# Layer 1 of a graph stack: row ends made per graph as small products of two one-hots and spread over the heads by DMA

## What is computed

```python
g_l = (h @ W_l.T).reshape(b, n, H, F)
g_r = (h @ W_r.T).reshape(b, n, H, F)
g_sum = g_r[:, :, None] + g_l[:, None]              # one vector for each pair (i, j)
e = einsum('bijhf,f->bijh', leaky_relu(g_sum, 0.2), w_attn)
e = where(adj == 0, -inf, e)
a = softmax(e, axis=j)
attn = einsum('bijh,bjhf->bihf', a, g_r)
out = leaky_relu(attn, 0.2)
```

## Time and profile before

| | |
|---|---|
| profiled execution | 1467.18 us |
| its span, first to last instruction | 1465.5 us |
| mean granted TensorE clock | 0.976 |
| PE busy | 1370.2 us, 93% |
| PE weight loads | 1154.1 us, 79% |
| DVE busy | 1150.3 us, 78% |
| ACT busy | 999.2 us, 68% |
| POOL (GpSimd) busy | 121.0 us, 8% |
| DMA queue of SP | 365.81 MB, 70.3% of 16 engines |

### The profile page before, as it was taken

How to read it: one execution, slowest core, us unless ns; L and a number is a source line. 1 busy time by engine, 2 the same in 40 slices (tenths; PEclk the granted TensorE clock), 3 DMA queues, 4 the chain that set the end, 5 groups by cost and what they waited for, 6 DMA issues and landing times. The chain is left out here.

```text
span 1465.5 us, 27752 instructions
## 1 busy us (share of the span) xinstructions
PE 1370.2 (93%) x9135; PEld 1154.1 (79%) x9194; DVE 1150.3 (78%) x2223; ACT 999.2 (68%) x2538; POOL 121.0 (8%) x259
## 2 busy tenths in 40 slices
PE   7984999999999999999999988799999999999867
PEld 6873666888888888888888887588888888888767
DVE  5875778787878878878788564589998989898967
ACT  5754878656566666666666421688888888888746
POOL 2011000000000000000000000000010001001176
PEclk9997999999999999999999999899999999999979
DMA  5202768878888888778788775788777877887234
GB/s 146 88 22 93 279 262 312 304 294 293 301 306 289 303 292 302 286 290 302 293 303 300 253 244 194 320 301 278 270 273 273 281 267 275 276 277 269 93 102 129
DMA packets 137586, 367.63 MB, mean 251 GB/s; under 512 B 12896, under 2 KB 71904, under 8 KB 137440
## 3 DMA queue, kind: packets, MB, share of 16 engines
q1 hardware_dynamic: 137440, 365.81, 70.3%
HBM read 231.54 MB, written 134.22 MB: 250 GB/s over the span
## 5 line engine op out<-in xcount | busy, mean ns | idle before, releaser
L967 DVE TENSOR_TENSOR b_wt<-bank,b_aT 128x512 f32<-128x512 f32 (+1 forms) x192 | 109.4, 599 | 99.2 <-PE bank L782 92.5
L1147 PE MATMUL wide<-W2c,c_h 128*128 128x128 f32 x1280 | 173.9, 275 | 3.0
L1147 PEld LDWEIGHTS wide<-W2c,c_h 128*128 128x128 f32 x1280 | 170.2, 193 | 3.3
L735 PE MATMUL wide<-b_vv,put_w 128*128 128x512 f32 (+1 forms) x384 | 170.9, 526 | 1.9 <-DVE b_vv L916 0.3
L757 PEld LDWEIGHTS bank<-b_wt,b_SITl 128*128 128x128 f32 x1280 | 156.4, 190 | 16.0 <-DVE b_wt L967 12.0
L757 PE MATMUL bank<-b_wt,b_SITl 128*128 128x136 f32 x1280 | 160.1, 280 | 9.4 <-DVE b_wt L967 9.4
L916 DVE TENSOR_TENSOR b_vv<-duo,b_vv 128x512 f32<-128x512 f32 (+1 forms) x192 | 114.1, 600 | 61.1 <-ACT b_vv L837 60.5
L782 PE MATMUL bank<-b_grl,b_SJl 128*128 128x128 f32 x1280 | 153.4, 275 | 1.0 <-ACT b_aT L844 0.6
L782 PEld LDWEIGHTS bank<-b_grl,b_SJl 128*128 128x128 f32 x1280 | 148.7, 192 | 4.8 <-issue 4.1
L1277 DVE TENSOR_REDUCE c_var<-c_ysq 128x4 f32<-128x512 f32 (+1 forms) x192 | 113.5, 591 | 42.4 <-ACT c_ysq L1206 42.3
L837 ACT ACTIVATE b_vv<-duo 128x512 f32<-128x512 f32 (+1 forms) x192 | 101.1, 526 | 45.8 <-PE duo L512 44.6
(11 more groups left out here) (223 smaller groups left out, 3013.0 us busy)
## 6 DMA issues: line engine op xcount, KB each, us to landing
si_d<-b_SI SPq DMA_DIRECT2D x64, 640.0 KB, 2.9
sj_d<-b_SJ SPq DMA_DIRECT2D x64, 640.0 KB, 4.1
sit_d<-b_SIT SPq DMA_DIRECT2D x64, 640.0 KB, 5.3
b_SJl<-sj_d SPq DMA_DIRECT2D x64, 640.0 KB, 5.8
b_SITl<-sit_d SPq DMA_DIRECT2D x64, 640.0 KB, 6.0
c_SJ<-sj_d SPq DMA_DIRECT2D x64, 640.0 KB, 5.4
c_SI<-si_d SPq DMA_DIRECT2D x64, 640.0 KB, 6.6
c_SIT<-sit_d SPq DMA_DIRECT2D x64, 640.0 KB, 4.2
```

The costliest lines, as they stand in the source:

```text
L735: pe.matmul(out, e.put_w[:, pos, :], vv[:, (pos + k) % 2, 0:width(k)], start=False, stop=(pos == R - 1)).then_inc(e_mm, 1)
L967: v.tensor_tensor(wt[:, mb, 4 * k:4 * k + rr, 0:P].rearrange("p r (h f) -> p r h f", h=HEADS), ring[k][:, 0:P * rr].rearrange("p (r h f) - ...
L1147: d = pe.matmul(bY[k][:, a:a + P], h[:, k, a:a + P], e.W2c[:, :], start=False, stop=(j == last))
```

## The change

- `put_m`, `mk` and `mark_rows` (line 742) go. `put_w` has 64 columns instead of 128. bE and `es` have 64 rows instead of 128, score(0) in the first step of a group starts the accumulation and waits for `es_ok`, which mark_rows waited for. The DVE subtraction of line 936 goes.
- The end of row i of a graph is a number between 1 and 1280. In step -1 five DVE instructions on 128 x 64 split it for all graphs into a block of 32 columns and a place in the block. For each group of 8 graphs POOL makes a one-hot of the block (`far`, 41 wide) and one of the place (`near`, 32 wide) for each graph, 16 instructions in all. PE multiplies them, `far` transposed times `near`: 41 x 32 for each graph, 8 matmuls in bf16 (`mark_ends`), in the step n % 8 = 0, ahead of score(2), into the unused columns 1280 to 1535 of `wide`. In the next step ACT multiplies by -MARK into `ends` (41 x 256).
- In its step n % 8 = 7 SP stores `ends` to DRAM (`mark_d`, 41 rows of 8 runs of 32 numbers). In its step n % 8 = 1 SP reads it back by 8 DMAs, each of which writes one graph's 1312 numbers to 8 partitions of `mark`. The forward scan of n % 8 = 1 waits for these (`mark_in`).
- Layer 3 uses the semaphores `x_in` of layer 0 again in place of four of its own.

```diff
+STEP = 32
+WHOLE = 1.5 * 2.0 ** 23
+ENDS = ECAP // STEP + 1
@@ layer0, gpsimd
-                pool.memset(e.put_m[:, :, :].bitcast(F32), 0.0).then_inc(flat_ok, 1)
-                q.add(pool.tensor_scalar(mk[:, :], mk[:, :], MARK, 1.0, ALU.mult, ALU.mult))
-                    q.add(pool.tensor_copy(e.put_m[:, k, H + HEADS * k:H + HEADS * (k + 1)],
-                                           mk[:, :].broadcast_to([P, HEADS])))
@@ layer1_packed
-        es = sb("es", [2 * H, ECAP])
-        mark = sb("mark", [H, ECAP + 1])
+        es = sb("es", [H, ECAP])
+        mark = sb("mark", [H, ENDS * STEP])
+        where = sb("where", [P, 2, B])
+        far = sb("far", [P, 2, R, ENDS], BF16)
+        near = sb("near", [P, 2, R, STEP], BF16)
+        ends = sb("ends", [ENDS, R, STEP])
+        bM = e.wide[0:ENDS, ECAP:ECAP + R * STEP].rearrange("a (g b) -> a g b", b=STEP)
@@ sync
+                    if pos == 7 and 0 < n < B:
+                        sp.wait_ge(ends_ok, K + 1)
+                        sp.dma_start(e.mark_v[:, R * K:R * K + R, :], ends[:, :, :]).then_inc(ends_out, 16)
+                    if soft(n, 1):
+                        sp.wait_ge(ends_out, 16 * K)
+                        if K > 1:
+                            sp.wait_ge(seq_z, 4 * K - 4)
+                        for k in range(R):
+                            sp.dma_start(mark[HEADS * k:HEADS * (k + 1), :],
+                                         e.mark_d[R * K - R + k, :].partition_broadcast(HEADS)).then_inc(mark_in, 16)
@@ gpsimd
+                pool.wait_ge(seq_m, 5)
+                for K in range(B // R):
+                    if K >= 2:
+                        pool.wait_ge(m_mm, K - 1)
+                    for k in range(R):
+                        i = R * K + k
+                        d = pool.tensor_scalar(far[:, K % 2, k, :], e.number1[:, 0:ENDS], where[:, 0, i:i + 1], 1.0,
+                                               ALU.is_equal, ALU.mult)
+                        d.then_inc(which_ok, 1)
...
@@ tensor
                     def score(k):
+                        if pos == 0 and k == 0 and n > 0:
+                            pe.wait_ge(es_ok, K)
                         pe.wait_ge(v_ok, 3 * n + k + 1)
-                        out = bE[:, chunk(k)]
-                        pe.matmul(out, e.put_w[:, pos, :], vv[:, (pos + k) % 2, 0:width(k)], start=False,
+                        pe.matmul(bE[0:H, chunk(k)], e.put_w[:, pos, :], vv[:, (pos + k) % 2, 0:width(k)], start=(pos == 0),
                                   stop=(pos == R - 1)).then_inc(e_mm, 1)
-                    def mark_rows():
-                        if pos == 0 and n > 0:
-                            pe.wait_ge(es_ok, K)
-                        for k in range(CHUNKS):
-                            pe.matmul(bE[:, chunk(k)], e.put_m[:, pos, :], s.SI[:, pos % 4, chunk(k)], start=(pos == 0), stop=False)
+                    def mark_ends():
+                        pe.wait_ge(which_ok, 2 * R * K + 2 * R)
+                        if K > 0:
+                            pe.wait_ge(ends_ok, K)
+                        for k in range(R):
+                            d = pe.matmul(bM[:, k, :], far[:, K % 2, k, :], near[:, K % 2, k, :], start=True, stop=True)
+                        d.then_inc(m_mm, 1)
...
                     if A:
+                        if pos == 0:
+                            mark_ends()
                         score(2)
@@ scalar
-                        act.copy(es[:, :], bE[:, 0:ECAP]).then_inc(es_ok, 1)
+                        act.copy(es[:, :], bE[0:H, 0:ECAP]).then_inc(es_ok, 1)
...
+                    if A and pos == 1:
+                        act.wait_ge(m_mm, K + 1)
+                        if K > 0:
+                            act.wait_ge(ends_out, 16 * K)
+                        act.mul(ends[:, :, :], bM[:, :, :], -MARK).then_inc(ends_ok, 1)
@@ vector
-                    if soft(n, 0):
+                    if soft(n, 1):
                         v.wait_ge(es_ok, K)
-                        v.wait_ge(pad_ok, 2)
-                        z.add(v.tensor_tensor(mark[:, 1:ECAP], es[H:2 * H, 1:ECAP], es[H:2 * H, 0:ECAP - 1], ALU.subtract))
+                        v.wait_ge(mark_in, 16 * R * K)
...
+                    if n == -1:
+                        q = Steps(v, seq_m)
+                        q.add(v.tensor_scalar(where[:, 1, :], e.end[:, :], 0.5 - 0.5 * STEP, 1.0 / STEP, ALU.add, ALU.mult))
+                        q.wait()
...
+                        q.add(v.tensor_tensor(where[:, 1, :], where[:, 1, :], e.end[:, :], ALU.add))
@@ adjacency_stack
-        put_w = sb("put_w", [P, 8, P])
-        put_m = sb("put_m", [P, 8, P], F32R)
+        put_w = sb("put_w", [P, 8, 8 * HEADS])
+        ends = nc.dram_tensor("mark_d", [B, ENDS, STEP], F32, kind="Internal").ap()
+        e.mark_v = ends.rearrange("g a b -> a g b")
+        e.mark_d = ends.rearrange("g a b -> g (a b)")
```

More of the change, by code:

```diff
@@ L609, in layer1_packed @@
         es_ok = sem("es_ok")
-        pad_ok = sem("pad_ok")
+        seq_m = sem("seq_m")
+        which_ok = sem("which_ok")
+        m_mm = sem("m_mm")
+        ends_ok = sem("ends_ok")
+        ends_out = sem("ends_out")
+        mark_in = sem("mark_in")
         seq_z = sem("seq_z")
@@ L708, in _ @@
                 pool.memset(s.junk[:, :], 0.0).then_inc(s.sq_ok, 1)
-                pool.memset(mark[:, 0:1], 0.0).then_inc(pad_ok, 1)
-                pool.memset(mark[:, ECAP:ECAP + 1], 0.0).then_inc(pad_ok, 1)
+                pool.wait_ge(seq_m, 5)
[8 more added lines that the diff above has]
+                    for k in range(R):
+                        i = R * K + k
+                        d = pool.tensor_scalar(near[:, K % 2, k, :], e.number1[:, 0:STEP], where[:, 1, i:i + 1], 1.0,
+                                               ALU.is_equal, ALU.mult)
+                        d.then_inc(which_ok, 1)
             @block.tensor
@@ L768, in step @@
                         if A:
-                            mark_rows()
                             score(0)
@@ L916, in bend @@
                         v.tensor_tensor(vv[:, b, 0:w], bU[b][:, 0:w], vv[:, b, 0:w], ALU.max).then_inc(v_ok, 1)
-                    z = Steps(v, seq_z, 5 * (K - 1))
+                    z = Steps(v, seq_z, 4 * (K - 1))
                     def forward(a, initial):
@@ L932, in step @@
                         bend(1)
-                    if soft(n, 0):
+                    if soft(n, 1):
                         v.wait_ge(es_ok, K)
-                        v.wait_ge(pad_ok, 2)
-                        z.add(v.tensor_tensor(mark[:, 1:ECAP], es[H:2 * H, 1:ECAP], es[H:2 * H, 0:ECAP - 1], ALU.subtract))
-                    if soft(n, 1):
-                        z.n = 1
-                        z.wait()
+                        v.wait_ge(mark_in, 16 * R * K)
                         if n > R + 1:
@@ L943, in step @@
                     if soft(n, 2):
-                        z.n = 2
+                        z.n = 1
                         z.wait()
@@ L947, in step @@
                     if soft(n, 3):
-                        z.n = 3
+                        z.n = 2
                         z.wait()
@@ L951, in step @@
                     if soft(n, 4):
[L952 removed]
+                        z.n = 3
                         z.wait()
@@ L1003, in step @@
                         select_rows(v, e, s, K, pos + 2, inner or n + 2 >= 4)
+                    if n == -1:
+                        q = Steps(v, seq_m)
+                        q.add(v.tensor_scalar(where[:, 1, :], e.end[:, :], 0.5 - 0.5 * STEP, 1.0 / STEP, ALU.add, ALU.mult))
+                        q.wait()
+                        q.add(v.tensor_scalar(where[:, 1, :], where[:, 1, :], WHOLE, None, ALU.add))
+                        q.wait()
+                        q.add(v.tensor_scalar(where[:, 0, :], where[:, 1, :], -WHOLE, 1.0, ALU.add, ALU.add))
+                        q.wait()
+                        q.add(v.tensor_scalar(where[:, 1, :], where[:, 0, :], -float(STEP), 1.0 + STEP, ALU.mult, ALU.add))
+                        q.wait()
+                        q.add(v.tensor_tensor(where[:, 1, :], where[:, 1, :], e.end[:, :], ALU.add))
                 every_step(v, step, LAG + 6)
@@ L1719, in layer3 @@
         junk = sb("junk", [P, G, P])
-        a_in = [sem(f"a_in{b}") for b in range(4)]
+        a_in, LOADED = e.x_in, 32 * (NG // 4)
         deg_ok, droot_ok, inv_ok, root_ok, all_ok, seq_a = (
```

12 lines of the change are left out of this document (3 added, 9 removed).

## The result

The change made the kernel slower: 1478.24 us, median of four runs (1477.34 to 1478.65), against 1467.10 for four runs of before (1465.88 to 1469.48). The ratio is 1.0073, 95% interval 1.006 to 1.0085. The prediction was 1444.0 with a range of 1435 to 1462, so both the sign and the range missed. The profiled execution of after took 1477.98 us, its span is 1475.9.

What follows compares the result with a forecast made beforehand. The prediction took PE to set the pace in the middle of layer 1, until the next engine is late. 14.1 + 8.7 + 2.2 + 0.2 - 1.8 = 23.4 us off 1467.18 gave 1443.8, stated as 1444, range 1435 to 1462.

Steps and rivals of the forecast that it cites:

- narrower put_w: Score weight loads of 64 columns instead of 128: can't be slower, worth 0 to 0.1 us in 13 early steps, taken as 0.
- early steps: Layer 1, steps 1 to 7 and 9 to 13: score(0) waits for bend(0) on DVE, so gain 0.
- Removed: mark_rows: Three matmuls fewer on PE per layer 1 step: up to 0.67 us, less where DVE isn't already waiting for bend(2).
- full-gain steps: 21 middle steps of layer 1 where DVE waits long enough ahead of bend(2): 0.67 us each, 14.1 us.
- tied ones: Middle steps n % 8 = 3 and 7, where DVE waits 0 or 0.15 us before bend(2): gains 0.1 and 0.25 us.
- Step 8: Layer 1: the es_ok wait moves to score(0), everything behind comes 0.65 us earlier; about 0.2 left after mark_ends.
- mark_ends: Eight added small PE matmuls in steps n % 8 = 0: 0.45 us, of which 0.15 disappears in a wait.
- Step -1 and step 0: Start of layer 1: five DVE instructions cost 1.2 us, POOL's one-hots 0.3; with mark_ends, 1.8 us lost.
- The store on one DMA engine: Rival: 41-row stores fall to one engine and delay SJl and grl in six steps, 30 us, 1474; chance 0.17.
- point of decision: Store time from which that rival decides: 23.4 / 6 + 4.5 = 8.4 us a store, 26 ns a packet.
- Read-backs: Eight added DMAs on SP, 3.8 to 9.5 us of issuing ahead of the loads; 3.8 hidden, 9.5 would not be.
- ACT, DVE line 936: ACT's added instruction in steps n % 8 = 1: 0, at most 3 us; removing DVE's subtraction in n % 8 = 0: 0.

Runs made afterwards that it cites:

- e1_wide: The changed kernel with put_w at 128 columns again (upper 64 zero), also writing 128 output rows; 1449.50 us.
- e2_before_narrow: The kernel before with only the scores' put_w narrowed to 64 columns in seven of eight steps, mark_rows kept; 1500.18 us.
- e4_no_marks: The kernel before without mark_rows and the subtraction of DVE line 936, nothing in their place, scores at 128 columns; 1440.82 us.
- e12_48_rows: e7_far128 with its one store of the marks a group padded from 41 to 48 rows; 1439.94 us.
- e6_early: e1_wide with the five small DVE operations moved from the end of step -1 to the start of layer 1; 1445.13 us.
- e7_far128: e6_early with the far one-hot padded from 41 to 128 columns; 1443.13 us.
- e10_two_stores: e7_far128 with the store of the marks made twice; 1478.74 us.
- e11_three_48: e7_far128 with the store of the marks made three times and padded from 41 to 48 rows; 1441.35 us.
- e9_three_stores: e6_early with the store of the marks made three times, the first two into spare memory; 1513.19 us.

## Why the prediction was wrong

**The step that failed: narrower put_w.** The prediction wrote that the load "can't be slower than now" and gave the edit 0 to 0.1 us in 13 early steps. The load isn't slower. What it missed is that the price of a load is not its own duration, but where it may start, and that the lower bound was set without a row of a 64 column load. e1_wide against after puts the term at 28.7 us, e2_before_narrow against before at 33; with it the forecast would have been 1444 + 29 = 1473. The rest are smaller misses: 1.4 us of the removal (26.1 against 27.5) and 4.6 of the added parts (8.7 against 4.1). Its range took a gain for the worst case where no row excluded a loss. The hint was in the earlier trace rows all the same: a load of 189 ns that lies "mostly under the matmul before" has its value from being covered, and an edit to its shape puts that cover at stake. The Trainium skill, TensorE: Matmul & The Clock Gate, section LDWEIGHTS (loading the stationary operand), lets a load's time go by its columns: the trace agrees. Where the two loads of a score follow at once, their starts lie 108 ns apart at 128 columns, 81 at 96, 62 at 72 and 55 at 64; the durations on record fall less (189, 163, 143, 134). Only the step's length goes the other way.

**Removed: mark_rows, and who is late in each step.** Right. e4_no_marks gave 1440.82 us where its expectation, built on the same terms, said 1440. In its middle steps the plain ones fell from 11.65 to 11.07 (0.58, where the prediction had 0.67 for most and 0.6 for n % 4 = 1), the steps n % 8 = 6 from 12.62 to 12.02 (0.60 against 0.67), and n % 8 = 3 and 7 to 11.23 (0.42, where it had 0.1 and 0.25). The full-gain steps were thus a little dear and the tied ones a little cheap. In e12_48_rows bend(2) has waits of 0.43, 0.68 and 1.28 us in some steps and none in others, as the per-step reading of the earlier trace rows supposed. The early steps gave nothing, as said (7.59 us against 7.53), with PE's wait for DVE of 0.8 at score(0) (0.9 forecast). Step 8 gave 0.64 (0.65 forecast), with the clock down in both executions.

**mark_ends.** 0.3 us net predicted, 0.2 measured in e1_wide, and 0 with loads of 128 columns.

**Step -1 and step 0.** 1.8 us predicted; 3.0 in after, of which about 1.0 is the width's, and in e1_wide 5.4 more than in e4_no_marks. The five operations were right (1.2 forecast, 1.1 measured). POOL's stall was taken as 0.3 from bounds of 0 to 4, and came to 1.0 in after and 2.8 in e1_wide. What no bound held is the granted clock behind the stall. All of it went when POOL started earlier (e6_early).

**The store on one DMA engine.** The rival was right that the 41 rows go in one line, but that was too cheap to matter. What it had as transfers waiting for their share of one engine is in the traces an issue that stands: SyncE is held for 5.35 us at the next load (e7_far128). Its point of decision, 8.4 us a store, was too high: at 8.0 us (e10_two_stores) 35.6 us were lost against e7_far128, as eight stores count and not six, and the clock fell behind five of them. The packet records of after have 328 packets of 128 bytes a store, 13 ns each (median), one behind the other for 4.1 us: the line through the two kinds of packet in the earlier trace rows said 13 ns and 4.3 us. "With 4.3 against 4.5 the room just holds" is what came: 4.8 us of room, one wait of 0.4 us at line 811 in the whole of layer 1:

```profile
PE bank L811 <- DMA b_grl<-gr_d: 0.4, 1, 0.4
```

The Trainium skill, DMA: Bandwidth & Descriptors, section Why a DMA increments its semaphore by 16 and not by 1, has the number of engines divide the slowest dimension. The trace agrees: 41 rows in one line, 48 rows not (e11_three_48). Its specifications have pieces below 512 bytes written by read-modify-write; at 13 ns for 128 bytes, what the line through the two longer kinds of packet gave, no price of that is seen here. That the result, 1478, lies near this rival's 1474 is an accident, as the 0.4 us of waiting show.

**Read-backs.** Predicted 3.8 us hidden in SyncE's slack. The eight take 4.0 us of issuing, and no wait for DMA follows them but one of 0.5 us in the first steps (e12_48_rows, line 812). Right.

**ACT, DVE line 936.** Nothing to see in either, as predicted.

After against before is then -26.1 (removal, e4_no_marks), +28.7 (width, after less e1_wide) and +8.7 (added parts, e1_wide less e4_no_marks). That these make +11.3 us where +11.1 was measured proves nothing, as the three differences lead from before to after by way of the same runs. That the width costs as much by itself is shown by e2_before_narrow, which holds none of the other parts.

## What to carry to other kernels

When an edit changes the shape of an operand, bound its price on both sides, also where the operation itself gets cheaper; here the weights were made narrower because nobody needed the other 64 columns, and the unneeded ones had held the loads under the matmuls. Padding was the cheap way out here: from 64 to 72 columns of weights, and from 41 to 48 rows of a transfer. And price a stall of PE above its length: behind waits of 2.8 to 7.0 us the granted clock mostly fell, behind waits of 1.8 to 1.9 in about half of the executions, for some 1.6 us more each time. Before a difference of a few us is put down to an edit, look whether such a fall stands in one trace and not in the other.

## What the runs showed of the hardware that was not expected

- With scores of 64 columns between operations of 128, the load of the score and the load behind it both begin only with their own matmuls (0.81 us of idle time ahead of the one behind in after). At 72, 96 and 128 columns both begin under the matmul that is running, the one behind 0.43 us ahead of its own. The cost was 0.44 to 0.65 us a step of six changes. Where the limit lies between 64 and 72 was not tried.
- The eight small products with 41 columns cost 0.2 us a time, with 128 columns none. Between 41 columns and the score's 64 in after no load was held (23 ns ahead of its matmul, as within the eight), so loads of 41 and 64 go together here, and those of 72, 96 and 128.
- While one engine drains a store, SyncE's queue stands at the next issue (5.35 us for one that takes 0.48), so one narrow store can hold up every transfer behind it even if they use other engines.
- The granted clock was 0.54 in the 4 us behind a wait of 7.0 us (e9_three_stores) and 0.60 behind one of 3.21 (e10_two_stores, 524.22 us), yet 1.00 behind one of 3.27 in the same execution (430.87 us). Behind the 1.84 us of step 8 it fell in e12_48_rows and not in e11_three_48. What decides it stays open.
